# First attention of a four-stage block: two more NF4 comparison planes as Sign on ScalarE

## The reference, cut to what matters

```python
# layer 0 attention, for each of 16 batches; t = 512 positions, 8 heads of 16
qkv = transpose(layernorm(x)) @ w_in.T + b_in
scores = q @ k.T / 4, where(|i - j| <= 64, scores, -inf); attn = softmax(scores)
o = transpose(attn @ v @ w_out.T + b_out)
x = x + einsum(relu(o) * encodings, w_ct) + b_ct

# the weights of the FFN behind it (3 x 1408 x 512, bf16): round trip through NF4
scaled = blocks / absmax_of_64                 # 64 values a block
idx    = argmin(abs(scaled - NF4))             # 16 levels, 15 thresholds between them
w      = NF4[idx] * dequantised_absmax
```

## Time and profile before

| | |
|---|---|
| median of 3 runs | 1548.59 us (1546.0 to 1550.63) |
| profiled execution | 1547.01 us, span 1545.2 us |
| busy over the span | PE 1365.3 us (88%), DVE 1022.3 us (66%), ACT 759.1 us (49%), POOL 216.4 us (14%) |
| the first attention | from the start to about 505 us of the span; its loop from about 63 to 489 us |
| granted TensorE clock | 1.00 throughout that loop after its first rounds |

### The profile page before, as it was taken

One profiled execution on the slowest core, in us unless ns is written; L12 is line 12 of the kernel. 1 busy time (PEld: TensorE's weight loads), 2 busy tenths in 40 slices (PEclk: granted clock), 3 DMA queues, 4 the chain that ended last, 5 costly groups with the idle time before them and its releaser, 6 DMA issues. The chain is left out here.

```text
span 1545.2 us, 28604 instructions
## 1 busy us (share of the span) xinstructions
PE 1365.3 (88%) x8664; PEld 820.9 (53%) x8664; DVE 1022.3 (66%) x3300; ACT 759.1 (49%) x1721; POOL 216.4 (14%) x252
## 2 busy tenths in 40 slices
PE   2579999999998899999889999997689899999894
PEld 0245555555554544444455565553333577777773
DVE  4889999999996545646446777777578555555210
ACT  4957777777766533332266666665410033333231
POOL 2010000000000000000020000000100145555453
PEclk7699999999999999999999999998799999999998
DMA  8344243433420300000000000000600488888884
GB/s 287 78 87 118 76 112 94 106 100 89 110 77 10 123 0 0 0 0 1 21 21 15 15 14 14 14 1 1 234 20 35 134 237 253 253 253 251 223 264 75
DMA packets 72167, 147.43 MB, mean 95 GB/s; under 512 B 10644, under 2 KB 40180, under 8 KB 67872
## 3 DMA queue, kind: packets, MB, share of 16 engines
q1 hardware_dynamic: 59728, 116.77, 24.6%
q0 software_dynamic: 12368, 29.77, 8.4%
HBM read 112.16 MB, written 34.34 MB: 95 GB/s over the span
## 5 line engine op out<-in xcount | busy, mean ns | idle before, releaser
L371 ACT ACTIVATE probs_t<-ps_sc 128x448 f32<-128x448 f32 x256 | 138.9, 543 | 108.4 <-PE ps_sc L512 106.7
L754 DVE CUSTOM_DVE_ANT_0 masked_scores<-ps_max,band_mask 128x192 bf16<-128x192 f32 (+1 forms) x512 | 177.1, 382 | 20.0 <-PE ps_max L492 15.0
L1166 PE MATMUL f_ps<-f_xt,w_t 128*128 (+1 forms) x704 | 158.5, 379 | 4.8 <-DVE f_xt L1111 2.4
L492 PE MATMUL ps_max<-k_stack,q_stack 96*128 96x192 bf16 (+1 forms) x512 | 95.7, 270 | 50.0 <-DMA k_stack<-dr_parts 24.0
L2599 DVE TENSOR_TENSOR d_inter<-d_silu_g,d_su 128x384 f32<-128x384 f32 x32 | 17.7, 554 | 171.2 <-PE d_su L2320 166.0
L1749 ACT ACTIVATE c_probs<-c_s,c_negmax 128x128 f32<-128x128 f32 x256 | 90.6, 366 | 59.5 <-DVE c_negmax L1834 58.7
L365 ACT ACTIVATE nf_above<-nf_scaled,nf_sign_at 128x512 f16<-128x512 bf16 x165 | 115.6, 713 | 0.0
L1166 PEld LDWEIGHTS f_ps<-f_xt,w_t 128*128 128x128 bf16 x704 | 68.8, 98 | 87.4 <-issue 4.4
L2187 POOL DMA_INDIRECT out<-d_h,d_scatter_now x64 | 97.3, 1521 | 104.1 <-DMA out<-d_h,d_scatter_now 87.3
L492 PEld LDWEIGHTS ps_max<-k_stack,q_stack 96*128 96x128 bf16 x512 | 44.7, 100 | 123.8 <-issue 54.4
L2482 DVE TENSOR_SCALAR d_onehot<-d_slot_no,d_pos 128x192 bf16<-128x192 bf16 x512 | 100.2, 284 | 0.0
(11 more groups left out here) (335 smaller groups left out, 2754.2 us busy)
## 6 DMA issues: line engine op xcount, KB each, us to landing
d_wgu<-in_ex_gu SPq DMA_DIRECT2D x32, 1024.0 KB, 5.6
d_wdown<-in_ex_d SPq DMA_DIRECT2D x32, 512.0 KB, 5.7
dr_parts<-qk_parts SPq DMA_DIRECT2D x32, 384.0 KB, 4.8
q_stack<-dr_parts SPq DMA_DIRECT2D x32, 192.0 KB, 3.0
k_stack<-dr_parts SPq DMA_DIRECT2D x32, 192.0 KB, 3.2
out<-x_sb SPq DMA_DIRECT2D x17, 256.0 KB, 2.6
nf_w<-in_nf_w POOLq DMA_DIRECT2D x3, 1408.0 KB, 15.8
q_stack<-dr_parts SPq DMA_DIRECT2D x32, 128.0 KB, 2.7
```

Source lines behind the costliest of these rows:

```text
L371: act.activation(pt[:, c, a:z], SP[c % 2][:].rearrange("p a w -> p (a w)")[:, a:z], ACT.Exp, scale=D0 ** -0.5).then_inc(s_e, 1)
L492: mm = pe.matmul(m[:, k, off:off + hi - lo], qst[0:96, b, h, BAND + qt * P:BAND + qt * P + P], kst[0:96, b, h, lo:hi], start=True, stop=True)
L754: op = dve.tensor_tensor_reduce(masked[:, c % 2, k, off:off + hi - lo], M[c % 2][:, k, off:off + hi - lo], mask[:, k, off:off + hi - lo], ...
L1166: mm = pe.matmul(bank[:], w12[:, m, kt, ft * P:(ft + 1) * P], xt[:, q, kt, bass.ds(g * N, N)], start=(kt == 0 and q == 0), stop=(kt == KT ...
```

## The change

Two planes, k = 8 and 9, go from VectorE to ScalarE in every chunk, so that VectorE makes eight and ScalarE seven. VectorE's compares occupy steps 0 to 3 instead of 0 to 4, and its fold stands at step 4 instead of 5. The table of Signs gets one more at each of four places per round: steps 1 and 5 of the first half, steps 1 and 4 of the second. (The planes' numbers shift, so the diff shows two whole lists.) In the tail, after the last round, ScalarE's loop over `range(NDV, NLV)` has seven Signs instead of five and VectorE's has two compares less. At the start, the constants for two more Sign planes are made (`half16`, `cut`, L802 and L803). `half16` and `cut` are allocated for seven planes instead of five.

```diff
-NDV = 10
+NDV = 8
@@
-    NF_INC = 6
+    NF_INC = 5
@@
-    SIGN_AT = [[[10], [11], [], [], [], [], [12], [13, 14]], [[10], [], [11], [], [], [12], [13], [14]]]
+    SIGN_AT = [[[8], [9, 10], [], [], [], [11], [12], [13, 14]], [[8], [9], [10], [], [11], [12], [13], [14]]]
@@ nf4_compare, on VectorE
-                if c < 5:
+                if c < 4:
                     for k in range(2 * c, 2 * c + 2):
                         op = dve.tensor_scalar(above[:, g, k, :], lvl[:, g, :], STEPS[k], LEVELS[k + 1] - LEVELS[k], ALU.is_gt, ALU.mult)
                     op.then_inc(s_ab, 1)
-                if c == 5:
+                if c == 4:
                     dve.wait_ge(s_ab, NF_INC * m + 4)
                     dve.tensor_tensor(above[:, g, 0:8:2, :], above[:, g, 0:8:2, :], above[:, g, 1:8:2, :], ALU.add).then_inc(s_ab, 1)
```

## The result

The changed kernel takes 1537.17 us (median of nine executions, 1534.53 to 1542.02); nine of the kernel before beside them take 1546.47 (1544.05 to 1550.63). The ratio is 0.994, with an interval of 0.9925 to 0.9955: 9.3 us less, 7.0 to 11.6 by the interval. That is faster, as forecast, but more than forecast: 1543.0 was predicted, and 1537.17 lies 0.8 us under the lower end of the range. The profiled execution took 1537.06 us for a span of 1535.3 us.

The account below looks back on a forecast made before the run. VectorE was taken to pace each round's first half up to the normalisation, TensorE the second up to ct. Loop -7.0 us plus tail +1.5 gives -5.5, from a median of 1548.59 to 1543 us; range 1538 to 1548.

Parts of the forecast that it names:

- Gain 0.1 us per round: Second half of a round: the saved pair only brings `gated` earlier, so ct starts sooner; 1.4 us over rounds 1 to 14.
- I take nothing there: Round 14: no gain counted, with plus or minus 2 us kept for a stall that comes or goes with code length.
- Gain 0.40 us per round: First half of a round: the saved pair lies in VectorE's unbroken stretch, so max_t comes earlier; 5.6 us over 14 rounds.
- the fold costs the same 1.13 us elsewhere: VectorE's fold, moved from step 5 to step 4 in each half, was taken to keep its 1.13 us cost.
- Tail "+1.5": Round 15 and the tail: later exps cost 0.3 us and two more exposed Signs before relu 1.2 us; range 1.2 to 2.5.
- Cost nothing: ScalarE's four added Signs per round, 2.4 us, each fall into an existing rest and do not lengthen the round.
- (0.76, the tightest: 0.15 us remain): First half, step 5: ScalarE's rest of 0.76 us before 216.02 takes the added Sign, leaving 0.15 us.
- 1.1 before it would start then: Second half, step 4: relu, 0.61 us later through the added Sign, still ends 1.1 us before the earlier start of `gated`.
- TensorE's idle before max_t shrinks from 0.67 to about 0.5: Sign to look for in a steady round: TensorE's wait before the second half's max_t falls from 0.67 to about 0.5 us.
- all of VectorE's time counts: Rival: every VectorE pair in both halves is worth 0.40 us, 11.3 us in all, giving 1537.3 us; chance 0.10.
- Nothing is left of it: Rival: a new wait eats the first half's gain or a 2 us code stall appears, 1545 to 1547 us; chance 0.27.
- ScalarE joins the chain: Rival: the second half's two new Signs cannot hide and delay ot_copy and relu, +12.8 us, 1561.4 us; chance 0.07.

Follow-up runs that it names:

- first half alone: The change made only in the even chunks' comparisons (and the last chunk, in the tail), odd chunks as in the kernel before; 1542.94 us, ratio 0.9978.
- Signs alone: The kernel before with four more Signs per round on ScalarE, into a tile nobody reads; 1546.87 us, ratio 1.0002.
- TensorE one matmul less: The changed kernel without plane 9's matmul in the sums of each second half (computation left out); 1535.23 us, ratio 0.9935.
- relief alone: The kernel before, VectorE leaving out planes 8 and 9 after round 0 and folding at step 4, no added Signs (computation left out); 1535.57 us, ratio 0.9927.
- second half alone: The change made only in the odd chunks' comparisons, even chunks and the last as in the kernel before; 1545.86 us, ratio 0.9998.
- relu after two Signs: The changed kernel with two of the tail's seven Signs ahead of the last relu and five behind it; 1535.31 us, ratio 0.9928.
- tail on VectorE: The changed kernel with the last chunk's seven Signs replaced by VectorE compares and their planes summed before ct; 1534.79 us, ratio 0.9925.
- fold at step 5: The changed kernel with VectorE's fold put back from step 4 to step 5; 1540.02 us, ratio 0.9951.
- VectorE's pair less: The changed kernel without VectorE's step 3 compares in the second half of every round but the first (computation left out); 1541.17 us, ratio 0.9962.

## Why the prediction was right in kind and wrong in size

The prediction missed by 1543.0 - 1537.2 = 5.8 us. 2.1 of these are the yardstick: three executions of before gave 1548.59 us, the nine beside the change 1546.47. The other 3.8 are the change: -9.3 by the timed runs (7.0 to 11.6) where the sum said -5.5.

The step that failed is the price of the second half. "Gain 0.1 us per round" stood there, the wait of ct for `gated` alone; the runs show 0.19 to 0.21, since ct's weight load came to lie under the matmul in front of it as well. Over 14 rounds that is about 1.4 us. The second step is "I take nothing there" for round 14, which got 0.8 us shorter. The ledger accounts for -7.3 in the stages that the change touches; the rest of the -9.3 is in "outside" and within the interval, and no run assigns it. Step by step:

- **"Gain 0.40 us per round" in the first half: right.** 0.42 measured, 0.39 with the first half alone. The late o_turn came as said: 212.07 - 211.52 = 0.55 us behind the sums' matmuls, against 0.44 before, and was absorbed. But "the fold costs the same 1.13 us elsewhere" hid a condition: with the fold left at step 5 the pair gives 0.26.
- **"Gain 0.1 us per round" in the second half: the mechanism right, the term mis-sized; it is 0.19 to 0.21.** I saw that ct waits for `gated`, and that TensorE paces the half; both are shown. I missed that ct, freed of the wait, also became 0.08 us shorter. This and the first half's 0.02 are the loop's difference: 14 rounds gave -1.2 - 7.5 = -8.7 us where -7.0 stood.
- **"In round 14 ... I take nothing there, and keep plus or minus 2 us for a stall": the bound right, the value off by 0.8.** Round 14 is 25.07 us with a stall of 2.01 before and 24.16 with 1.25 after: 23.06 and 22.91 without it. So some 0.15 us are the relief's, and the other 0.7 come from a stall that the change happened to shorten: luck, as far as the forecast goes.
- **Tail "+1.5": right.** From the last max_t to relu it is 498.18 - 471.39 = 26.79 us before (26.80 again) and 488.93 - 460.52 = 28.41 after (28.45 and 28.42): +1.62 for a forecast of 0.3 + 1.2. It splits as forecast: 0.4 us in round 15 and 1.2 between ot_copy and relu. Seven Signs took 488.93 - 484.65 = 4.28 us for a forecast of 4.3. The stage as a whole came out 2.2 us longer; the other 0.6 go with TensorE's clock, and nothing shows that the change has a part in them. From relu on the executions fall in two groups, with five Signs and with seven alike: 7.6 to 7.9 us at a mean granted clock of 0.78 or 0.79 (before twice, Signs alone, changed once, TensorE one matmul less), and 8.5 to 9.2 us at 0.62 to 0.65 (relief alone and second half alone, with the old five Signs; changed twice and three others with seven). Both of before fell in the shorter group.
- **"Cost nothing" for ScalarE: right in the steady rounds,** shown by the Signs alone and by the relief alone. But "(0.76, the tightest: 0.15 us remain)" is wrong as to which is tightest: the working set each rest against one Sign and left out that max_t comes closer by 0.4 us and the late o_turn pushes the exps by 0.2. The rest before ot_copy, 0.57 us in the forecast, is used up. relu's distance to `gated` was also off: the "1.1 before it would start then" takes the first half's 0.40 us from `gated` and not from relu. 229.29 - 0.40 - 227.44 is 1.45 us, and 224.26 - 222.69 = 1.57 us were measured.
- **"TensorE's idle before max_t shrinks from 0.67 to about 0.5": wrong place.** It is 0.63; the 0.43 us of the wait at step 1 went in its stead.
- **Chance.** Of the 5.8 us, the mis-sized terms of the loop make 1.7. The yardstick (2.1), the stall (0.7) and the 2 us that no stage accounts for are the larger part, and TensorE's clock in the tail (0.6) worked against them.

Of the rivals, "all of VectorE's time counts" gave 1537.3 us, and the time came out at 1537.17, but its mechanism is refuted. It needed the second half shorter by 0.40 us per round, and that is 0.19 to 0.21; a further pair of VectorE's there gives nothing, and one matmul of TensorE's gives its full price. The agreement is luck: the yardstick, the stall and the small terms add up to it. The rule of the Trainium skill (Perfetto Trace Analysis, Identifying the Most-Contended Engine) that went with that rival is to relieve the engine with the highest occupancy first. This case agrees in part: VectorE had the highest, 25.41 us per round against 24.89, and relieving it gave its full price in one half of the round; in the other, TensorE set the pace. "Nothing is left of it" and "ScalarE joins the chain" are refuted by the halves.

With the terms as measured, the sum would have been -8.7 - 0.8 + 2.2 = -7.3 us, 1541.3 from the three runs shown, and 1539.2 from the nine. The last 2 us to 1537.17 stay open.

## What to carry to other kernels

When two engines are both above 90% busy, cut the period at the handovers between them and ask for each part who paces it: an instruction is worth its full price in one part and nothing in the next. Where a wait of 0.1 us in front of a matmul goes, look in the same trace for that matmul where it waits for nothing, and count its own shortening too; here it was 0.08 us on top of 0.11. When an engine is relieved, set the rests of the others against the new times and not the old: with the relief alone, the rest in front of ot_copy lost 0.6 us though ScalarE had not one instruction more. And take the yardstick from more than three executions if the forecast gain is under 1%: here the median of three was off by 2.1 us, nearly 40% of the gain that I forecast.

## What the runs showed of the hardware that was not expected

**TensorE's clock in the first rounds.** The windows of round 0's first half, of the changed kernel (third execution) and of the one with a matmul less in the second halves; the clock granted is the third figure from the end, and 1.00 means the upper level, 2.4 GHz, throughout:

```profile
63.87:79.16 15.29, 12.83 (x77) 7.23 (x76) 13.21 (x55) 12.93 (x24) 0.84 (x1) 0.83 0.10 26
```

```profile
64.44:78.40 13.96, 11.26 (x78) 6.66 (x76) 13.13 (x56) 12.76 (x24) 0.84 (x1) 0.93 0.11 28
```

This half has the same instructions in both, and took 1.3 us less with the clock at 0.93 than at 0.83; TensorE's busy time is 1.6 us less. In round 1 the same again, 14.08 us at 1.00 against 15.72 at 0.89. These 3.0 us are nearly the whole of why rounds 0 and 1 took 56.6 us there and 58.6 to 61.4 elsewhere, and why they are a poor place to read a gain from. Why the clock rose earlier in that execution was not tried.

**A stall with no visible cause.** In round 14, the first behind the hardware loop, VectorE stands still once for something that the profile doesn't show: 2.01 and 1.97 us before, 1.85 with the Signs alone, 2.06 with the second half alone, 2.47 with the first half alone, 1.25, 1.41 and 1.29 in the changed kernel, 1.29 to 1.50 in four kernels close to it (relief alone, relu after two Signs, tail on VectorE, TensorE one matmul less), 1.41 with the fold at step 5, 2.45 with VectorE's pair less. It repeats to 0.2 us for a kernel and differs by up to 1.2 between kernels, so it goes with the code. A few packets on the queues for instructions are seen within 3 us of it, but what it waits for was not tried and stays open.

**Long and short rounds in the loop.** The hardware loop repeats two rounds in one turn, and the second-half stretches alternate: 12.12 and 12.02 us in the changed kernel, 12.38 and 12.19 before (12.34 and 12.20 again). It is not the jump back that costs the difference. The long stretch lies inside a turn (from round 4 to 5, for instance), and the short one holds the jump (from 5 to 6). In the changed kernel TensorE is level in both up to the last scores, and add_x starts 1.2 us behind ct in both; then max_t waits 0.61 us for add_x inside a turn and 0.51 over the jump, as the first max_t of round 7 shows beside that of round 6 above:

```profile
253.52 0.27 PE L498 MATMUL ps_g<-ident,row_max 128*16 128x128 f32 x1 [0.61 <-DVE x_sb L785]
```

VectorE does pay something at its own jump, 0.18 us between add_x and the next take_max, but the first half behind it is as long either way (14.06 us). Why max_t follows add_x later inside a turn stays open.
